# Queries and keys of a first attention layer projected in transposed half blocks, rotated there, and placed head by head with DMA

## The reference

```python
q = apply_rope(proj(Wq)); k = apply_rope(proj(Wk)); v = proj(Wv)   # 16 heads of 16
scores = einsum('bhqd,bhkd->bhqk', q, k) / sqrt(16)
scores = where(causal, scores, -inf)
out = einsum('bhqk,bhkd->bhqd', softmax(scores), v)
return einsum('btd,ed->bte', out, Wo)
...
# apply_rope: a head's first 8 columns x1 and last 8 x2
x1 * cos - x2 * sin, x1 * sin + x2 * cos
```

## Time and profile before

| | us |
|---|---|
| median of 3 runs | 476.17 (474.27 to 481.29) |
| the profiled execution, device time | 478.39 |
| its span in the trace | 475.8 |
| PE busy in the span | 454.6 (96%) |
| DVE busy | 352.2 (74%) |
| ACT busy | 254.0 (53%) |
| POOL busy | 228.3 (48%) |

### The profile page before, as it was taken

One profiled execution on the slowest core, in us unless ns is written; L12 is line 12 of the kernel. 1 busy time (PEld: TensorE's weight loads), 2 busy tenths in 40 slices (PEclk: granted clock), 3 DMA queues, 4 the chain that ended last, 5 costly groups with the idle time before them and its releaser, 6 DMA issues.

```text
span 475.8 us, 10572 instructions
## 1 busy us (share of the span) xinstructions
PE 454.6 (96%) x3166; PEld 360.9 (76%) x3166; DVE 352.2 (74%) x1182; ACT 254.0 (53%) x679; POOL 228.3 (48%) x222
## 2 busy tenths in 40 slices
PE   7999999999999998989999799999999998999996
PEld 4855999999999997667666466488888876666685
DVE  6994988888886666678998579887667755554796
ACT  3273233333333336899999624656666655732731
POOL 0704667777774310766760000276666654077730
PEclk9699999999999999799999889999999999999999
DMA  8907988888888871387785460036666699433321
GB/s 255 394 2 234 325 261 272 266 261 269 266 263 257 269 252 59 99 244 182 173 194 176 132 235 1 21 114 180 176 178 178 177 136 132 115 95 104 101 77 66
DMA packets 42549, 85.51 MB, mean 180 GB/s; under 512 B 7008, under 2 KB 27792, under 8 KB 41856
## 3 DMA queue, kind: packets, MB, share of 16 engines
q1 hardware_dynamic: 31456, 60.98, 38.2%
q0 software_dynamic: 9888, 22.82, 21.7%
q10 hardware_dynamic: 1152, 1.05, 0.6%
HBM read 67.25 MB, written 17.56 MB: 178 GB/s over the span
## 4 chain that ended last, share of the span: by engine, by line
PE 74%; ACT 10%; DVE 9%; DMA 4%; issue 3%; DVEq 0%
PE ps L905 18%; PE ps L938 14%; PE ps L909 8%; PE ps L798 6%; ACT til L667 6%; PE ps L1086 6%; PE ps L890 5%; DMA til<-xn_rows,gidx 3%; PE ps L1097 3%; PE ps L1063 2%; PE ps L920 1%; PE ps L991 1%; PE ps L1156 1%; ACT stk L562 1%; PE ps L934 1%
## 5 line engine op out<-in xcount | busy, mean ns | idle before, releaser
L467 POOL DMA_INDIRECT til<-xn_rows,gidx x110 | 110.9, 1008 | 155.2 <-PE ps L890 74.3
L618 ACT ACTIVATE til<-ps 128x256 f32<-128x256 f32 x110 | 42.1, 383 | 120.4 <-PE ps L890 120.4
L905 PEld LDWEIGHTS ps<-til,experts 128*128 128x128 f32 x752 | 91.1, 192 | 3.9 <-ACT til L618 0.8
L905 PE MATMUL ps<-til,experts 128*128 128x128 f32 x752 | 91.8, 275 | 1.2 <-ACT til L618 0.6
L938 PE MATMUL ps<-experts,til 128*128 (+1 forms) x314 | 87.9, 386 | 0.2
L938 PEld LDWEIGHTS ps<-experts,til 128*128 128x128 f32 (+1 forms) x314 | 50.9, 190 | 9.2 <-issue 3.9
L639 ACT ACTIVATE til<-ps,wtile 128x256 f32<-128x256 f32 x110 | 51.5, 468 | 2.5 <-PE ps L938 2.3
L909 PE MATMUL ps<-experts,til 128*128 x252 | 52.5, 331 | 0.0
L667 ACT ACTIVATE til<-til,mxs 128x128 f32<-128x128 f32 (+1 forms) x128 | 49.8, 458 | 0.0
L890 PE MATMUL ps<-cst,til 128*128 128x128 f32 x220 | 42.7, 275 | 1.8 <-DMA til<-xn_rows,gidx 1.8
L1396 DVE CUSTOM_DVE_ANT_0 til<-ps,cst 128x128 f32<-128x128 f32 (+1 forms) x128 | 37.9, 353 | 6.4 <-PE ps L991 5.4
(11 more groups left out here) (207 smaller groups left out, 852.1 us busy)
## 6 DMA issues: line engine op xcount, KB each, us to landing
experts<-in_gu SPq DMA_DIRECT2D x47, 512.0 KB, 4.9
sorted_rows<-til SPq DMA_DIRECT2D x110, 128.0 KB, 3.3
experts<-in_gu SPq DMA_DIRECT2D x8, 768.0 KB, 4.8
experts<-in_dn SPq DMA_DIRECT2D x4, 1024.0 KB, 11.0
experts<-in_dn SPq DMA_DIRECT2D x8, 384.0 KB, 6.0
til<-xn_rows,gidx POOLq DMA_INDIRECT x110, 4.2
xr<-in_x SPq DMA_DIRECT2D x2, 512.0 KB, 4.1
xn_rows<-xn ACTq DMA_DIRECT2D x8, 128.0 KB, 9.9
```

Source lines behind the costliest of these rows:

```text
L467: po.indirect_dma_start(xg[:, t % 4, :], None, xn_dram[s.n], bass.IndirectOffsetOnAxis(ap=gidx[:, t:t + 1], axis=0))\
L618: ac.activation(xgT[:, j % 2, :, :], ps[:, j % 2, 0:D].rearrange("p (k t) -> p k t", k=KD), ACT.Copy)\
L905: mm = pe.matmul(ps[:, b0, m * P:(m + 1) * P], gw[:, j, k * w + m * P:k * w + (m + 1) * P], xgT[:, j % 2, k, :], start=(k == 0), stop=(k = ...
```

## The change

- `wide` swaps its operands in the first layer: a 128-column block of weights is stationary, 512 tokens are moving. The columns are first sorted on POOL by two copies into `wqk_halves`: all heads' first halves (8 columns each) in one block, all second halves in another. The result `qkT` has features on partitions.
- `rotate` works on `qkT` (four POOL instructions for 128 tokens as before), with tables for 256 positions that a new 512 KB load brings; it runs after every third tile.
- SP issues 64 DMAs (`place_heads`), four with each of tiles 16 to 23 and 28 to 35, each moving 8 partitions x 2 x 512 elements of `qkT` to the partitions where `scores` reads them, `heads_qk`.
- `turn_stack` and `stack` go, with the waits on their semaphores. `vst` holds all values, is cleared by POOL at tile 41 and filled by ACT in eight copies (`value_columns`) with the last eight tiles; `values` goes from the pairs.
- A group is now four neighbouring heads, so `turn_back` writes its result without a permutation.
- Since `heads_qk` lies where the second block's gate-up weights go, SP's loads of these are put in another order and the last three wait for the last scores.

```diff
+        qkT = att[:, 0:4096].rearrange("p (f w t) -> p f w t", f=2, w=2)
+        vst = att[:, 0:4096].rearrange("p (t h d) -> p t h d", t=NTT, h=HEADS)
+        heads_qk = [big[:, at:at + 4096].rearrange("p (w q t) -> p w q t", w=2, q=4) for at in (4096, 8192)]
...
+                def place_heads(n):
+                    half, q, r, f = n // 32, n // 8 % 4, n // 2 % 4, n % 2
+                    if n % 32 == 0:
+                        sp.wait_ge(s_rope, NTT // 2 * (half + 1))
+                    head = HALF * (4 * q + r)
+                    sp.dma_start(heads_qk[half][32 * r + HALF * f:32 * r + HALF * (f + 1), :, q, :],
+                                 qkT[head:head + HALF, f, :, half * 512:(half + 1) * 512]).then_inc(s_heads, 16)
...
                 for t in range(s.NT + 2):
                     if s.n == 0 and t + 4 < s.NT:
                         tile_weight(t + 4)
+                    if s.n == 0 and (16 <= t < 24 or 28 <= t < 36):
+                        for n in range(4):
+                            place_heads((t - 16 if t < 24 else t - 20) * 4 + n)
...
-                    if s.n == 0 and t % 4 == 3 and t // 4 <= NTT:
-                        rotate(t // 4 - 1, (t // 4 - 1) % 2, t // 4 - 1)
+                    if s.n == 0 and t >= 7 and (t - 7) % 3 == 0 and (t - 7) // 3 < NTT:
+                        rotate((t - 7) // 3)
+                    if s.n == 0 and t == 41:
+                        po.wait_ge(s_heads, 16 * 64)
+                        po.memset(vst[:, :, :, DH:DH + 1], 1.0).then_inc(s_vst, 1)
+                        po.memset(vst[:, :, :, DH + 1:], 0.0).then_inc(s_vst, 1)
...
+            po.wait_ge(s_wqkv, 16)
+            for w in range(2):
+                link(po.tensor_copy(wqk_halves[:, :, w, :, :].rearrange("p k f (h d) -> p k f h d", d=HALF),
+                                    wqkv_sb[:, :, w * D:(w + 1) * D].rearrange("p k (h f d) -> p k f h d", f=2, d=HALF)))
...
-            run_pairs([(6, 8, values(1)), (-1, 2, lambda n, j: stack(n, j) if n >= 2 else None), (13, 8, gate_tanh), (1, 1, probs(1)), (2, 1, probs_turned_act),
-                       (-1, 8, values(0)), (8, 4, turned0), (0, 1, probs(0)), (4, 2, attended)])
+            run_pairs([(13, 8, gate_tanh), (1, 1, probs(1)), (2, 1, probs_turned_act),
+                       (8, 4, turned0), (0, 1, probs(0)), (4, 2, attended)])
...
                 for k in range(KD):
+                    if s.n == 0:
+                        mm = pe.matmul(ps[:, 4 + i % 4, :], wqk_halves[:, k, i % 2, i % 4 // 2, :], s.xnT[:, k, i // 4 * 512:(i // 4 + 1) * 512],
+                                       start=(k == 0), stop=(k == KD - 1))
...
-            run_pairs([(-1, 2, lambda n, j: turn_stack(n, j) if n >= 2 else None), (0, 2, lambda n, j: scores(n, j) if n >= 1 else None), (2, 1, turn_probs), (8, 4, turn_rows),
+            run_pairs([(0, 2, lambda n, j: scores(n, j) if n >= 1 else None), (2, 1, turn_probs), (8, 4, turn_rows),
```

More of the change, by code:

```diff
@@ L59, in constants @@
     freq = (np.float32(1.0) / np.float32(10000.0) ** (np.arange(half, dtype=np.float32) / np.float32(half))).astype(np.float32)
[L61 to L67, removed]
+    ang = (np.arange(SEQ, dtype=np.float32)[None, :] * freq[np.arange(P) % half][:, None]).astype(np.float32)
+    for w, scale in ((0, -np.float32(DH) ** -0.5), (1, np.float32(1.0))):
+        c[:, C_COS + w * SEQ:C_COS + (w + 1) * SEQ] = np.cos(ang) * scale
+        c[:, C_SIN + w * SEQ:C_SIN + (w + 1) * SEQ] = np.sin(ang) * scale
     c[:, C_PMOD:C_PMOD + 1] = p % 32
@@ new lines, in gather_tiles, with rotate @@
+                        po.wait_ge(s_rtab, 16)
+                    if s.n == 0 and t >= 7 and (t - 7) % 3 == 0 and (t - 7) // 3 < NTT:
[4 more added lines that the diff above has]
+                        po.memset(vst[:, :, :, DH + 1:], 0.0).then_inc(s_vst, 1)
+            def rotate(i):
+                here, at = slice(i * P, (i + 1) * P), slice(i % 2 * P, (i % 2 + 1) * P)
+                ct, st = (rope_cs[:, c, :, at].unsqueeze(1).broadcast_to([P, 2, 2, P]) for c in range(2))
+                raw = qkT[:, :, :, here]
+                po.tensor_tensor(rtmp, raw, st, ALU.mult).then_inc(s_rst, 1)
+                po.wait_ge(s_rst, 2 * i + 1)
+                po.tensor_tensor(raw, raw, ct, ALU.mult).then_inc(s_rst, 1)
+                po.wait_ge(s_rst, 2 * i + 2)
+                po.tensor_tensor(raw[:, 0, :, :], raw[:, 0, :, :], rtmp[:, 1, :, :], ALU.subtract)
+                po.tensor_tensor(raw[:, 1, :, :], raw[:, 1, :, :], rtmp[:, 0, :, :], ALU.add).then_inc(s_rope, 1)
+                po.wait_ge(s_rope, i + 1)
@@ L610, in turn_and_project, with value_columns @@
                     wide(s, i)
+            def value_columns(i):
+                if i == 0:
+                    ac.wait_ge(s_vst, 2)
+                ac.activation(vst[:, i, :, 0:DH], v_rows[:, i, :].rearrange("p (h d) -> p h d", d=DH), ACT.Copy).then_inc(s_vst, 1)
             def tiles(s):
@@ L640, in weigh @@
                       .then_inc(s.y_ready, 1)
-                    if s.n == 0 and t in (NT0 - 4, NT0 - 3):
-                        stack(t - (NT0 - 4), 0)
+                    if s.n == 0 and 0 <= t - (NT0 - 8) < NTT:
+                        value_columns(t - (NT0 - 8))
                     if s.n == 0 and t == NT0 - 3:
@@ L670, in probs @@
                 return work
-            def values(half):
-                def work(b, j):
-                    if b > 0:
-                        ac.wait_ge(s_pv, 4 * b + 2 * half - 2)
-                    ac.activation(vst[:, half, :, :, 0:DH], v_rows[:, bass.ds(b * 2, 2), HALF * DH * half:HALF * DH * (half + 1)]
-                                  .rearrange("p t (h d) -> p t h d", d=DH), ACT.Copy).then_inc(s_vst, 1)
-                return work
             def probs_turned_act(p, j):
@@ L791, in wide @@
             def wide(s, i):
+                if i == 0 and s.n == 0:
+                    pe.wait_ge(s_pool, 3)
                 if i < 4:
@@ L1039, in turn_back @@
                 pe.wait_ge(s_otr, 2 * m + 2)
-                pe.wait_ge(s_stk, min(2 * m + 5, 4 * BATCH))
                 if m >= 1:
```

98 lines of the change are left out of this document (35 added, 63 removed).

## The result

The changed kernel takes 487.47 us in the median of four runs (485.38 to 494.9), the kernel before 476.5 (474.27 to 481.29): a ratio of 1.0189 with an interval of [1.0135, 1.0243], so 6 to 12 us slower.

What follows compares the result with a forecast made beforehand. PE bounds the tiles; ACT, PE and DVE, all within 2.1 us of the 19.54 us batch, bound the attention. 478.39 - 4.3 - 0.5 - 0.9 + 0.1 = 472.8 us profiled, median 2.2 lower: 470.5, range 466 to 481.

Steps and rivals of the forecast that it cites:

- SP's room for the head transfers: In the tiles, SP is free for 2.08 us and four issues take 1.9, so they just fit.
- slack: In the tiles, a weight load lands 3.8 us before the gate-up product that reads it, hiding overruns.
- Rival 1: In the tiles, eight-partition head transfers are slow on DMA engines, PE waits: 492 us, chance 0.15; in part 473 to 482, 0.15.
- The attention: Relieving ACT and PE cuts a batch from 19.54 to 18.2 us: gain 4.3 us, plus 0.5 at the pairs' start.
- Both waits of DVE: In an attention batch, DVE waits 0.8 us for `project0`, kept, and 0.8 us for `turn_back`, expected to go.
- the floor that I named: In the attention, DVE's busy time of 17.43 us a batch, below which the period can't go.
- The front: Ahead of the tiles, POOL's column copies overlap a few more DVE routing instructions: 0 to 0.5 us, taken as 0.1.
- POOL's wait at tile 41: POOL waits for the 64 transfers and clears 1920 elements of a partition, 2 us; some 6 us are free.
- Rotation on POOL, `wide`, the tables, the order of the second block's loads: First block's start and tiles, and second block's loads: all hidden, no cost, 0 to 1 us for contention with gathers.
- Rival 3: In the attention, three engines wait for each other in turn, period above 19 us: 473.5 to 475 us, chance 0.12.
- rival 2: In the attention, ACT was nearly all of it; period 17.0 us, gain 9.5, total 466.5 us, chance 0.08.
- The transposes of the first groups in the tiles: Two quads of PE transposes for groups 0 and 1 leave the tiles: gain 0.9 us.

Runs made afterwards that it cites:

- first and third kernels: First: changed kernel, head transfers cut to 1 KB, ratio 1.0241 to the kernel before; third: changed kernel, ACT issuing two of each tile's four, 0.9859.
- sixth kernel: Changed kernel with column copies on ACT and two of each tile's four head transfers issued by ACT: 471.04 us, ratio 0.9824 to the kernel before.
- fifth kernel: Changed kernel with the two column copies moved from POOL to four copies on ACT: 488.22 us, ratio 1.0169 to the kernel before.

## Why the prediction was wrong

Forecast 470.5 us (466 to 481), measured 487.47.

- **The step that failed: SP's room for the head transfers.** "Four issues at the 0.42 to 0.47 us of its short ones at the start are 1.9. It just fits" (into 2.08 us). An issue took 0.69 and four 2.9, the loop 4.05 us for 2.98, and 4.57 in every fourth turn. The right row was not there to be read: no transfer of the trace before went from SBUF to SBUF. But then the price was unknown, and I bounded the engines' price from both sides and SP's not at all. The sum had nothing for it, and it cost 14.1. It had 0.18 us of room in 2.08, and the prediction said itself that it would fail at over 2.1. This was a rival that should have had its own chance and price: at 0.69 us, 8 x 1.07 = 8.6 us a burst, less 3.8 of slack, twice: 9.6. The measured bursts overran by more, 9.8 and 10.7 us (33.66 and 34.54 us for eight turns of 2.98), because of the fourth turns and of two loads whose issue took 1.01 and 0.69 us. Of these 20.5 us the tiles lost 14.1, so slack hid about 6.4 of the 7.6 that two bursts should have had.
- **The fourth turn** was in the trace of before, too. There SP is free for 1.74 us, from 96.97 to 98.71, and not for 2.08, so that the 1.9 us of the prediction didn't fit even at its own price (timeline of SP, before):

```profile
96.64 0.33 SPq L400 DMA_DIRECT2D experts<-in_gu  x1
98.71 0.33 SPq L408 DMA_DIRECT2D sorted_rows<-til  x1
```

- **Rival 1** had the sign and the place (PE waiting for `experts<-in_gu`) but not the mechanism. Its own test was landing times well above 4.7 us; they are 4.5. The first and third kernels settle it: 13.0 us were lost without the bytes, and 0.9 with all of them, though the DMA engines were then busy for 0.90 of the time. What one transfer costs the engines wasn't measured.
- **The attention** was right in its mechanism and too low in size. Forecast 4.3 + 0.5, with a period of 18.2; measured 6.9, with a period of 17.44. Both waits of DVE left, where I had kept the one behind `project0`. It falls on the floor that I named (17.43), and in part that is luck: DVE's own busy time for its 83 instructions fell from 17.43 to 17.11 and 0.33 us of gaps fill the rest. ACT (16.61 for 16.4) and PE (16.34 for 16.6) came out as worked out from the earlier trace rows.
- **The front** was mis-sized: 0.1 us, at most 0.5, and it was 2.4. The column copies took 1.45 us for the two, near the 1.2 estimated. What I had left out is that they push the bias work onto other instructions of DVE (0.7 us), and that PE ran its narrow products at the lower clock for longer (the other 1.7 us). The copies bring the loss and taking them away cures it; how they bring the clock's part isn't shown.
- **POOL's wait at tile 41** was put at some 6 us that are free. It was 9.0 us, since the last transfer went out only at 174.1, and the clearing took 1.8. It cost PE little here, a wait of 0.3 us at 185.22, for PE had itself been kept waiting by late weights until 179.97.
- **Rotation on POOL, `wide`, the tables, the order of the second block's loads**: nothing, as said. A rotation from 92.76 leads to the next gather at 97.30, 4.5 us. From the first narrow product of the second block to the end it is 189.6 us, 189.8 before.
- **Rival 3** (new coupling in the attention) did not happen; **rival 2** comes near what the sixth kernel shows (a gain of 8.0 in the attention, where the rival had 2.5 x 3.25 = 8.1), but its mechanism failed: the period stayed on DVE's floor of 17.4 and did not go to 17.0.
- **The transposes of the first groups in the tiles** (0.9 us) can't be told apart from the rest: the sixth kernel's tiles take 140.9 us for 140.2, its first scores come 143.0 us after its first gate-up product, for 142.8. So no run shows the 0.9 us.

## What to carry to other kernels

A queue that issues for a tight loop has a budget of its own: add up the issues of one turn and compare with the period, before asking whether the data engines have room. Where a DMA is of a kind that the trace does not have yet, its issue time is as unknown as its bandwidth and wants a bound; from SBUF to SBUF it was twice that of a load. Take the longest turn for it and not the usual one: here every fourth had 0.5 us more to do. When such a loop overflows, deal the issues out to a second queue that has room: here the same 64 transfers cost 14 us on one queue and less than 1 on two.

## What the runs showed of the hardware

- SP needs 0.60 to 0.73 us to issue a DMA from SBUF to SBUF, with 8 to 128 partitions and 32 to 1024 elements in each, against 0.30 to 0.34 for a load or a store in a steady loop. The dear ones are those with SBUF as source and target: 8x2x512 out of HBM took 0.30 us. A store right behind head transfers took 0.43 or 0.44. On ACT's queue the transfers cost the same (0.70 us each), and in the third and sixth kernels the tiles bore two of them.
- SP's loop goes by 1.13 + 0.73 us for each transfer: 4.05 with four, 3.33 with three, 2.60 with two (the loads at 108.87 and 111.47 of the sixth kernel), all three measured. The last is under the tile's 2.98; the two kernels with two lose 0.9 and 0.7 us in their tiles.
- A bf16 copy of 768 elements on POOL held up an instruction of DVE with two operands in SBUF to its end: 0.83 us for 0.17 (one row before, two after, one in the fifth kernel). It doesn't take every instruction of POOL: beside the tensor-tensor one that begins at 14.37 in the trace of before, the same DVE instruction took 0.18, from 14.38 on.
- The clock of the ten microseconds from 290 us on was 0.51 in one execution and 1.00 in another, with the same products of PE and a wait of 0.61 or 0.21 us ahead of them. 2.4 us of lead were gone with it. The wait doesn't decide: a third execution (the sixth kernel) had 0.81 us and a clock of 1.00. What does stays open.
